# GpSimd sets future keys to zero after the exponentials, in place of a TensorE mask product on the transposed scores

## The reference, cut to what matters

```
att = einsum('bhtd,bhsd->bhts', q, k) / sqrt(D)
att = att + (tril(rel) + causal)[None] * slopes   # rel = key place - query place, causal = -inf for future keys
att = softmax(att, axis=-1)
y = einsum('bhts,bhsd->bhtd', att, v) @ W_proj + b_proj
```

## Time and profile before

| | |
|---|---|
| median of three runs | 2239.19 us |
| profiled execution | 2248.01 us, of which its span 2245.0 |
| mean granted TensorE clock | 0.955 of full speed |
| PE busy over the span | 2036.9 us (91%), 15073 matmuls |
| DVE, ACT, POOL busy | 1597.1 (71%), 1366.8 (61%), 860.3 (38%) |
| DMA moved | 160.39 MB |

### The profile page before, as it was taken

One profiled execution on the slowest core, in us unless ns is written; L12 is line 12 of the kernel. 1 busy time (PEld: TensorE's weight loads), 2 busy tenths in 40 slices (PEclk: granted clock), 3 DMA queues, 4 the chain that ended last, 5 costly groups with the idle time before them and its releaser, 6 DMA issues.

```text
span 2245.0 us, 45058 instructions
## 1 busy us (share of the span) xinstructions
PE 2036.9 (91%) x15073; PEld 1729.1 (77%) x15073; DVE 1597.1 (71%) x3576; ACT 1366.8 (61%) x3150; POOL 860.3 (38%) x967
## 2 busy tenths in 40 slices
PE   4999989999999999987058999999969999999998
PEld 2888779999999999973056788777747777777776
DVE  4666658888888888767964656667657777777775
ACT  2666556666666666657844566677745555555554
POOL 2111134444444444420012211144426666566665
PEclk9999999999999999988578999989979999999999
DMA  4333500000000000000003333445413333333333
GB/s 138 115 110 108 144 1 1 2 1 1 2 1 2 1 1 2 1 1 1 0 22 109 110 102 101 115 141 153 110 67 121 125 121 119 120 128 117 120 121 102
DMA packets 138973, 160.39 MB, mean 71 GB/s; under 512 B 15293, under 2 KB 99325, under 8 KB 138493
## 3 DMA queue, kind: packets, MB, share of 16 engines
q1 hardware_dynamic: 137740, 157.13, 23.3%
q10 hardware_dynamic: 1008, 0.45, 0.1%
HBM read 119.09 MB, written 38.44 MB: 70 GB/s over the span
## 4 chain that ended last, share of the span: by engine, by line
PE 70%; issue 8%; POOL 7%; DVE 6%; ACT 4%; SPq 2%; DMA 2%; POOLq 0%; ACTq 0%; DVEq 0%
PE bank L835 7%; POOL h_lo L1951 6%; PE bank L253 5%; PE bank L799 5%; PE bank L801 5%; PE bank L800 5%; PE bank L1670 5%; PE bank L846 5%; PE bank L1672 4%; PE bank L1671 4%; PE bank L264 4%; PE bank L233 3%; PE bank L251 3%; PE bank L232 3%; PE bank L1574 2%
## 5 line engine op out<-in xcount | busy, mean ns | idle before, releaser
L1951 POOL TENSOR_TENSOR h_lo<-h,h_hi 128x512 fp32r<-128x512 f32 x264 | 341.0, 1292 | 244.4 <-ACT h_hi L1771 244.2
L475 DVE TENSOR_REDUCE nm<-bank 128x4 f32<-128x512 f32 (+1 forms) x384 | 238.1, 621 | 230.4 <-PE bank L233 227.5
L1200 POOL TENSOR_TENSOR pw<-ew,rw 128x410 f32<-128x410 f32 x256 | 225.6, 881 | 369.2 <-DVE rw L1059 356.7
L393 ACT ACTIVATE pt<-bank 128x512 f32<-128x512 f32 (+1 forms) x384 | 227.8, 597 | 144.8 <-PE bank L253 144.3
L1764 ACT ACTIVATE sl<-bank 128x512 f32<-128x512 f32 x264 | 157.9, 598 | 239.5 <-PE bank L1672 237.0
L955 ACT ACTIVATE ew<-bank,nmax 128x205 f32<-128x205 f32 x512 | 216.8, 431 | 133.5 <-DVE nmax L1051 133.5
L1892 DVE TENSOR_TENSOR bank<-bank,sl 128x512 f32<-128x512 f32 x264 | 184.2, 698 | 149.6 <-PE bank L1672 120.6
L253 PE MATMUL bank<-q_pack,k_diag 128*128 128x128 f32 (+1 forms) x1536 | 259.8, 293 | 0.1
L253 PEld LDWEIGHTS bank<-q_pack,k_diag 128*128 128x128 f32 (+1 forms) x1536 | 208.3, 181 | 26.9 <-issue 11.7
L835 PE MATMUL bank<-kvt,qs 128*128 128x205 f32 x1024 | 221.5, 339 | 0.0
L1670 PE MATMUL bank<-x_hi,w_hi 128*128 128x512 f32 x528 | 210.4, 399 | 0.0
(11 more groups left out here) (321 smaller groups left out, 5369.6 us busy)
## 6 DMA issues: line engine op xcount, KB each, us to landing
share_b<-share_rows SPq DMA_DIRECT2D x256, 256.0 KB, 3.1
q_rows<-q_hi SPq DMA_DIRECT2D x96, 128.0 KB, 2.7
q_pack<-q_rows SPq DMA_DIRECT2D x32, 384.0 KB
k_rows<-k_hi SPq DMA_DIRECT2D x64, 128.0 KB, 2.1
raw<-in_experts SPq DMA_DIRECT2D x33, 192.0 KB, 3.2
q_rows<-q_lo SPq DMA_DIRECT2D x48, 128.0 KB, 2.8
q_pack<-q_rows SPq DMA_DIRECT2D x32, 192.0 KB
k_diag<-k_rows SPq DMA_DIRECT2D x128, 48.0 KB
```

The lines of the kernel that those rows point to most:

```text
L393: nc.scalar.activation(m.pt[0:a.keys, c, :, :].rearrange("p h t -> p (h t)"), m.flip[c % 2][0:a.keys, :], ACT.Exp).then_inc(s.exped.semaph ...
L475: nc.vector.tensor_reduce(m.nm[:, u % 2, :].rearrange("p (h c) -> p c h", c=NC)[:, c, :], m.score[c % 2][:, 0:HC * a.columns].rearrange("p ...
L1200: nc.gpsimd.tensor_tensor(m.pw[:, k, :, 0:KW], m.ew[:, k, :, :], m.rw[:, k, :].unsqueeze(2).broadcast_to([128, 2, KW]), ALU.mult)\
L1951: nc.gpsimd.tensor_tensor(m.h_lo[:, k % 3, :], m.h[:, (k + u) % 2, :], m.h_hi[:, k % 3, :].bitcast(F32), ALU.subtract).then_inc(s.los, 1)
```

## The change

The transposed scores get no mask product: L251 goes, in attention 0 and attention 1, 128 times in each. In its place GpSimd runs `affine_select` in place on each group's exponentials, 128 keys x 512, after `exped` and before `weigh`, which now waits for `selected`: where the query place is at least the key place the value stays, else it is 0. In GpSimd's body the four selects stand between the operations that were there. The position term of attention 0, which was part of `alibi_t`, becomes a key row: the second row of each head's maxima rows in `k_diag` holds key place x slope, and the query side of it is a 1. So the maxima are kept as one rounded row (VectorE's L475 writes float32r into `nmx`), the second row of `nmx` is set to 1 once, and the rounding and the rest (L484, L486) go, in all three attentions. `nmx` is double. The slope rows are copied from an input to a DRAM tensor and from there into the four slots of k_diag0, five DMAs on SP's queue before attention 0; the loads of `alibi_t` and `causal_t` go. The mask product of `scores` (L232) stays.

```diff
     def transpose_maxima(a, b, values_before):
-        wait(pe, a.s.max_split, b + 1)
+        wait(pe, a.s.maxed, NC * b + NC)
...
     def scores_t(a, b, u, c):
...
-        if a.mask is not None:
-            nc.tensor.matmul(bank[:], m.ident_b[:], a.mask_t(c), start=True, stop=False)
         for h in range(HC):
             last = nc.tensor.matmul(bank[0:a.keys, 128 * h:128 * h + 128], a.keys_of_head(b, c, h),
-                                    a.queries(b, c), start=a.mask is None, stop=a.mask is None or h == HC - 1)
+                                    a.queries(b, c), start=True, stop=True)
...
     def weigh(a, b, u, c):
         s, j = a.s, NC * b + c
-        wait(pe, s.exped, j + 1)
+        wait(pe, s.selected if a.causal else s.exped, j + 1)
...
-    def maxima(a, b, u, c):
+    def maxima(a, b, c):
...
-            wait(dve, s.max_split, b - 1)
-        nc.vector.tensor_reduce(m.nm[:, u % 2, :].rearrange("p (h c) -> p c h", c=NC)[:, c, :],
+            wait(dve, s.max_t, b - 1)
+        nc.vector.tensor_reduce(m.nmx[:, b % 2, :, 0, c],
...
-    def split_maxima(a, b, u):
...
-        nc.vector.tensor_copy(m.nmx[:, :, 0, :], nm).then_inc(s.max_hi.semaphore, 1)
...
-        nc.vector.tensor_tensor(m.nmx[:, :, 1, :], nm, m.nmx[:, :, 0, :].bitcast(F32), ALU.subtract)\
-            .then_inc(s.max_split.semaphore, 1)
...
+    def select(b, c):
+
+        wait(pool, a.s.exped, NC * b + c + 1)
+        probs = m.pt[:, c, :, :]
+        nc.gpsimd.affine_select(probs, probs, [[0, HC], [1, T]], ALU.is_ge, 0.0, base=0, channel_multiplier=-1)\
+            .then_inc(a.s.selected.semaphore, 1)
+
     def body(b, u):
+        if a.causal:
+            select(b, 0)
         if place(a, b + 1):
             widen_values(*place(a, b + 1), u + 1)
+        if a.causal:
+            select(b, 1)
+        if tail is not None:
+            tail(b)
         if u % 2 == 1 and place(a, b - 1 + a.ahead):
             query_lows(*place(a, b - 1 + a.ahead))
+        if a.causal:
+            select(b, 2)
+        if u % 2 == 1 and place(a, b - 1 + a.ahead):
             key_lows(*place(a, b - 1 + a.ahead))
+        if a.causal:
+            select(b, 3)
         if u % 2 == 1 and place(a, b + 1 + a.ahead):
             add_base(*place(a, b + 1 + a.ahead))
...
                 sp.wait_ge(m.s.filled, 1)
+                sp.wait_ge(m.s.sloped, 16)
+                for u in range(SLOTS):
+                    sp.dma_start(m.k_diag0[DATA:128, u, :, :, :].rearrange("r h c t -> r (h c t)").bitcast(F32),
+                                 alibi_rows).then_inc(m.s.sloped, 16)
```

More of the change, by code:

```diff
@@ L63, with __init__ @@
 class Attention:
-    def __init__(self, keys, cross, paired, first_value, split_weights, measures_context, mask, mask_t, wq, wk, wv, wo, bq, bk, bv, base):
+    def __init__(self, keys, cross, paired, first_value, split_weights, measures_context, causal, mask, wq, wk, wv, wo, bq, bk, bv, base):
         self.keys, self.cross, self.first_value, self.split_weights = keys, cross, first_value, split_weights
         self.paired, self.ahead = paired, 8 if paired else 6
-        self.measures_context, self.mask, self.mask_t = measures_context, mask, mask_t
+        self.measures_context, self.causal, self.mask = measures_context, causal, mask
         self.columns = keys + keys % 2
@@ L109 @@
     NAMES = ("normed", "based", "transposed", "inputs_t", "keyed", "queries", "keys", "query_lows", "key_lows",
-             "packed", "valued", "values", "widened", "scores", "maxed", "max_hi", "max_split", "max_t", "max_s",
-             "scores_t", "exped", "weighted", "sums_s", "sums_t", "recips", "heads_out", "heads_t", "heads_s",
+             "packed", "valued", "values", "widened", "scores", "maxed", "max_t", "max_s",
+             "scores_t", "exped", "selected", "weighted", "sums_s", "sums_t", "recips", "heads_out", "heads_t", "heads_s",
              "projected_out", "updated", "measured", "loaded0", "loaded1", "loaded2", "loaded3")
@@ L139, in __init__ @@
         self.exped = count("exped", NC * B)
+        self.selected = Count(sem["selected"], (0, NC * B, 2 * NC * B)[stage])
         self.weighted = count("weighted", NC * B)
@@ L343, in attention_tensor @@
         scores(a, 2, 2, 0)
+        pe.wait_ge(m.s.sloped, 16 * SLOTS + 16)
         scores_t(a, 0, 0, 0)
@@ L542, in body @@
             if c < NC - 1 and place(a, b + 2):
-                maxima(*place(a, b + 2), u + 2, c + 1)
+                maxima(*place(a, b + 2), c + 1)
             elif c == NC - 1 and place(a, b + 3):
-                maxima(*place(a, b + 3), u + 3, 0)
-            if c == 2 and place(a, b + 2):
-                split_maxima(*place(a, b + 2), u)
+                maxima(*place(a, b + 3), 0)
             if tail is not None and isinstance(b, int):
@@ L551, in attention_vector @@
     if a.earlier is None:
+        nc.vector.memset(m.nmx[:, :, :, 1, :].bitcast(F32), 1.0)
         normalise(a, 0)
@@ L561, in attention_vector @@
         for c in range(NC):
-            maxima(a, 0, 0, c)
-        split_maxima(a, 0, 0)
+            maxima(a, 0, c)
         values(a, 4)
@@ L566, in attention_vector @@
         for c in range(NC):
-            maxima(a, 1, 1, c)
-        split_maxima(a, 1, 1)
+            maxima(a, 1, c)
         for q in range(6, a.ahead, 2):
@@ L571, in attention_vector @@
             normalise(a, q + 2)
-        maxima(a, 2, 0, 0)
+        maxima(a, 2, 0)
     over_sequences(body)
@@ L622, in body @@
             fill_later(b)
-        if tail is not None and isinstance(b, int):
-            tail(b)
     if a.earlier is None:
@@ L2315, in program @@
             m.v_store0 = over("v_store0", [128, B * C])
-            m.alibi_t = over("alibi_t", [128, H * T], BF16)
+            m.unused_alibi = over("unused_alibi", [128, H * T], BF16)
             m.alibi = over("alibi", [128, H * T], BF16)
@@ L2363, in program @@
             keys=T, cross=False, paired=True, first_value=True, split_weights=False, measures_context=False,
-            mask=lambda c: m.causal[:], mask_t=lambda c: m.causal_t[:],
+            causal=True, mask=lambda c: m.causal[:],
             wq=m.w3[:, 0:128], wk=m.w3[:, 128:256], wv=m.w3[:, 256:384], wo=m.w3o[:],
@@ L2367, in program @@
         cross = Attention(
-            keys=L, cross=True, paired=True, first_value=False, split_weights=True, measures_context=False, mask=None, mask_t=None,
+            keys=L, cross=True, paired=True, first_value=False, split_weights=True, measures_context=False, causal=False, mask=None,
             wq=m.w4q[:], wk=m.w4kv[:, 0:128], wv=m.w4kv[:, 128:256], wo=m.w4o[:],
@@ L2592, in constants @@
     causal = np.repeat(hidden[:, None, :], HC, 1)
-    causal_t = np.repeat(hidden.T[:, None, :], HC, 1)
     alibi = at[None, :] * slope[:, None]
     alibi = np.where(future[:, None, :], np.float32(MASKED), alibi[None])
-    alibi_t = alibi.transpose(2, 1, 0)
     blocks = np.zeros((128, RING, HC, NC), np.float32)
+    alibi_rows = np.zeros((HC, 2, NC, HC, NC, T), np.float32)
     for j in range(HC):
         for c in range(NC):
-            for k in range(2):
-                blocks[DATA + (j * 2 + k) * NC + c, :, j, c] = 1.0
+            blocks[DATA + j * 2 * NC + c, :, j, c] = 1.0
+            alibi_rows[j, 0, c, j, c] = 1.0
+            alibi_rows[j, 1, c, j, c] = at * slope[c * HC + j]
     def fresh(n):
```

25 lines of the change are left out of this document (9 added, 16 removed).

## The result

The kernel after takes 2216.8 us against 2242.4 before, measured side by side (medians of 19 runs each); the ratio is 0.9901, with a 95% interval of 0.9878 to 0.9925. The direction came out, the size did not: 25.6 of the 43.5 us by the medians, half by the ratio. The time lies inside the stated range, near the 2213 of rival 3. The times of the kernel after also spread more, from 2209.4 to 2239.6, where those of the kernel before lie between 2237.3 and 2251.1.

The account below looks back on a forecast made before the run. TensorE's queue was taken to bound both self-attentions. Attention 0 17, attention 1 24.5 and cross-attention 4, less 2 for the selects, gave 43.5 us: 2239.2 - 43.5 = 2195.7 us, range 2180 to 2235.

Parts of the forecast that it names:

- rival 3: Attention 0 gives nothing, since SyncE's chain at its longest (16.0 us) holds every pair near 14.8: 2213 us, chance 0.12.
- Attention 0, the step that failed: Removing the mask product saves 17 us (12 to 25) in attention 0, limited by SyncE's chain.
- the chain: SyncE in attention 0, from scores_t(b,3) through load, saves and landings to the rows of b+5: 14.8 to 16.0 us.
- on average half of the excess: TensorE's wait for SyncE in attention 0, averaged at 0.35 to 0.95 us, making a pair of sequences 13.8 us.
- The selects: Four added on GpSimd per sequence, 0.95 us each (ends 0.6 and 1.3), not binding by throughput.
- The size of a mask product: TensorE's product in scores_t, taken as 0.20 us, between 0.14 and 0.28, 128 times in each self-attention.
- the 2 us for them: Total cost put on the added selects, for the hops where they are short.
- the slack before the products: Time between exponentials and the products with the values: 1.32 us for group 1, 1.43 for group 3; a select fits.
- rival 1: Selects of 1.3 us and more outlast the slack by about 0.2 us a sequence: 2209 us, chance 0.13.
- Rivals 1 and 2: Selects on GpSimd late but not the bound (2209 us, chance 0.13), or the bound, kernel slower (2280 to 2357, chance 0.17).
- One row: Two VectorE operations fewer before transpose_maxima: 4 us in the cross-attention (0 to 8), nothing in the self-attentions' steady part.
- The start: Five more DMAs before attention 0 cost 1 us; the shorter way to the first transposed maxima gives the same back.

Follow-up runs that it names:

- e9: The kernel after again, no edit, for a second profile and second set of times: 2214.0 us, ratio 0.988 to the kernel before.
- e3: The kernel after with a product of identity and zeros put back before scores_t in attention 0 alone: 2214.7 us, ratio 0.9862 to the kernel before.
- e5: The kernel before with only the maxima kept as one rounded row, mask products as before: 2232.9 us, ratio 0.9954 to the kernel before.
- e4: The kernel after without the 256 selects, so the result is wrong: 2207.0 us, ratio 0.9831 to the kernel before.
- e6: The kernel after with the query saves ahead of the load for b+4 and without selects (wrong result): 2201.1 us, ratio 0.9805 to before.
- e7: The kernel after with the early query saves and every select done twice: 2246.0 us, ratio 1.002 to the kernel before.
- e1: The kernel after with the three query saves ahead of the load for b+4 at odd b in attention 0: 2202.9 us, ratio 0.9814 to before.
- e8: The same kernel as e1, run again: 2205.0 us, ratio 0.9837 to the kernel before.

## Why the prediction was wrong

1. **Attention 0, the step that failed.** The prediction named the chain, its length (14.8 to 16.0 us) and that TensorE would wait for it. It then priced a wait at its own length, halved ("on average half of the excess"), and took a pair of 13.8 us; measured were 15.1 in the first profile of after and 14.1 in e9. Of the 17 us for this stage nothing came in the median run (e3, e5). Two things were missing. Two waits of 2.0 and 2.3 us were followed by a clock at its lower level for about 10 us each, which made pairs of 18.7 and 18.8. And the landing of the last save, 2.1 us in nearly all places, took 4.1 and 3.0 us just ahead of these two waits. In e9 the last save of a pair landed in 2.1 us every time, the clock hardly fell, and the 31 sequences gained 10.8 us. The first copy of queries for the wide stage, which follows, came 16 us earlier there (302.7 to 286.7); in e5, with the masks still in, it came at 293.4, so not all of that is due to the mask. The selects are a second part of the loss, see 3. Rival 3 (attention 0 gives nothing, 2213) was thus near the measured time, with a chance of only 0.12. It had the chain at 16.0 us in every pair as its reason, and not the clock.
2. **The size of a mask product.** Attention 1 went from 233.4 to 212.8 us. Add the 1.5 us of the selects and take off the 2.2 of the row: 19.9 us for 124 products, 0.16 each, where 0.20 was taken. The timelines show where the rest stays. Two of a sequence's four `scores_t` stand behind a weighing, and there the way from the start of the 16 products to the start of `scores` went from 1.21 us (1294.63 to 1295.84) to 1.08 (1297.44 to 1298.52), only 0.12 to 0.13 less. The other two lose 0.21: from the transposes of xn to the start of `scores` it was 0.83 (1299.68 to 1300.51) and is 0.62 (1302.01 to 1302.63). The mean of the four is the 0.16 above. TensorE's timeline of attention 1, after and then before:

```profile
1297.44 0.64 PE L261 MATMUL bank<-pt,vx 128*32 128x128 f32 x16
1298.02 0.66 PE L250 MATMUL bank<-q_pack,k_diag 128*128 128x128 f32 x4
1298.52 0.39 PE L231 MATMUL bank<-causal,ident_b 128*128 128x512 bf16 x1
...
1302.01 0.38 PE L193 MATMUL bank<-ident,xn 128*128 128x128 f32 x2
1302.15 0.64 PE L250 MATMUL bank<-q_pack,k_diag 128*128 128x128 f32 x4
1302.63 0.39 PE L231 MATMUL bank<-causal,ident_b 128*128 128x512 bf16 x1
```

```profile
1294.63 0.64 PE L264 MATMUL bank<-pt,vx 128*32 128x128 f32 x16
1295.21 0.39 PE L251 MATMUL bank<-causal_t,ident_b 128*128 128x512 bf16 x1
...
1295.84 0.39 PE L232 MATMUL bank<-causal,ident_b 128*128 128x512 bf16 x1
...
1299.68 0.38 PE L194 MATMUL bank<-ident,xn 128*128 128x128 f32 x2
1299.90 0.38 PE L251 MATMUL bank<-causal_t,ident_b 128*128 128x512 bf16 x1
...
1300.51 0.39 PE L232 MATMUL bank<-causal,ident_b 128*128 128x512 bf16 x1
```

3. **The selects** are shorter than taken (0.636 us), and TensorE's products waited for them 1.1 us in the whole of after (below 3 was forecast; the row of its waits below) and its weight loads 4.4. But the 2 us for them, of which attention 1 shows 1.5, was too small: without them the kernel is 8 to 12 us faster (e4), with the early saves 1 to 4 (e6). With one select the slack before the products was enough, as said. Beyond its edge the price was too low: at 1.3 us a group e7 lost 0.8 us a sequence in attention 1, in place of the 0.2 of rival 1, since GpSimd's queue at odd b is then full. The rule of the Trainium skill, GPSIMD Engine Reference, "Performance pitfalls for Q7 kernels", 1.03 to 2.03 cycles an element or 0.44 to 0.87 us, holds the measured value; the 5.1 us of a branching body did not come. Rivals 1 and 2, which need a select of 1.3 us and more, fall.

```profile
PE bank L261 <- POOL pt L600: 1.1, 4, 0.4
```

4. **One row** was mis-sized the other way: 10 us (7 to 13 by the interval of e5) where the sum had 4. Some 4.5 of it are in the cross-attention and 2.2 in attention 1, for which the prediction had nothing; the rest can't be placed. Without this luck the kernel after would have been further from the forecast.
5. **The start**: TensorE's first scores came at 34.7 us against 34.3, as good as nothing.

What stays open is why a landing of a save takes 3 to 4 us at times, what else than its length decides whether a wait brings the clock down, and how the selects cost what e4 gives back. Late landings are not new with the change: between 60 and 240 us the longest of a save of q_rows is 3.5 us before, 3.4 in e4 and 5.4 in e6, all three without selects. What differs is where they fall and whether TensorE's queue still covers them.

The version that beats both and still computes the right result is e1 (e8): the change with the saves of the queries ahead of the load, 0.9814 and 0.9837 of the kernel before.

## What to carry to other kernels

When work is taken from the busiest engine, measure how much room the next chain has, DMA issues and landings included, and take its worst case, not its mean. A wait that is new on TensorE is to be priced with the clock that it may cost afterwards: here two of 2.0 and 2.3 us cost some 5 us each. For an operation put on another engine, count that engine's work in its fullest body, not in the mean. And look at the order on the DMA queue first: here three saves moved ahead of one load were worth 10 to 16 us by the medians, against the 20 us that the mask product gave in attention 1.

## What was not expected of the hardware

Waits of nearly the same length did different things to the granted clock: 1.9 us in after and 1.7 in e9 left it at 1.00, 2.0 and 2.3 in after were followed by 0.50 for some 10 us each, and 1.6 in e9 by 0.50 for some 3 us. A 128x512 float32 `affine_select` takes 0.626 to 0.647 us. A save of 128 KB of key rows that lands in 2.1 us in most cases took up to 4.1 in after.
